# Routed experts in tiles of 512 rows instead of 256, with the down-projection turned round

## The chip, the cores and the metric

The kernel runs on one core of one Trainium2 chip. The metric is the device time of one launch in microseconds (us), lower is better. Times within one core are counted from the first instruction of the profiled execution.

## The reference, cut to what matters

The model has two layers, each with a mixer and a mixture of experts, on x of shape (32, 256, 128) in float32. The change concerns the first layer's experts alone: 8192 tokens of 128 values, 8 experts, each token sent to its two best experts.

```python
x = hidden_states.reshape(-1, H)              # 8192 x 128
logits = x @ gate_w                           # 8 experts
mult, sel = _sparse_mixer_routing(logits)     # two experts a token, a weight for each
w = jnp.sum(mult[:, :, None] * (sel[:, :, None] == jnp.arange(E)[None, None, :]), axis=1)
h = jax.nn.silu(jnp.einsum('th,ehf->etf', x, w1)) * jnp.einsum('th,ehf->etf', x, w3)   # F = 512
out = jnp.einsum('etf,efh,te->th', h, w2, w)
```

## The kernel before

The kernel is a sequence of stages, with a barrier over all engines between them. Four of them bear on the change.

- `ffn_front` computes the router's choices and scatters 16384 rows (two a token, each of 128 values, a destination and a weight) into the table `slot_inputs` in HBM, one region for each expert. GpSimd issues the 128 scatters. The scatter sorts the rows by expert. SyncE writes pad rows, `TOK` of them (256), behind each expert's last row (L871, 8 transfers at addresses that it reads from a table), and `TOK` rows for each tile in excess (L864, 7 transfers). A chain of small VectorE operations on one partition (L1078 to L1095) works out which expert and which row each tile begins at.
- `experts0` runs over a fixed number of tiles of `TOK` rows: `2 * NT // ROWS0` full ones, where NT is 64, and E - 1 = 7 more, because each expert's last tile may be partly empty. With `ROWS0 = 2` that is 64 + 7 = 71 tiles. All of them are computed whether they hold rows or padding.
- `combine0` reads the two results of each token back and adds them to the residual.
- The stages of the second layer follow, and share no code with the change apart from `ROWS0` and `TOK`, which they do not use.

One tile of `experts0` works as follows. SyncE loads its rows (`e_x`, L1132) and its expert's three weight matrices (`e_w`, 768 KB, L1133) up to four tiles ahead. TensorE turns the rows with two transposes (L1151) into PSUM; ScalarE copies them out as `e_xT` (L1190). The hidden width of 512 is worked through in two halves of 256. In each half TensorE multiplies two 128x128 blocks of w1 (L1174) and two of w3 (L1178) with the 256 columns of `e_xT`; ScalarE takes silu of the first (L1197); VectorE multiplies it with the second, giving `e_g` (L1208). In the down-projection (L1161) `e_g` is the stationary operand and a block of w2 the moving one, 128 columns at a time, so that the result has rows on the partitions. VectorE scales it by the row's weight (`e_y`, L1215) and copies the destinations (L1214). GpSimd scatters each 128 rows with an indirect transfer (L1224). The down-projection of a half is emitted one half late, so that TensorE has other work while silu and the product are made. Every engine's order is written out by hand. The waits are on semaphores: `at` and `upto` wait for a count, `upto` on semaphores that start at one.

Of the kernel before, what the change touches and what calls it, by code (L numbers as in the profile page):

```python
# [13 lines left out]
P = 128  # L14
# [626 lines left out]
FC = F // P  # L641
STAGES = 4
CAP = 80
ROWS0 = 2
TOK = ROWS0 * P


# [157 lines left out]
def ffn_front(core, layer, rows, H, XS, background, pad, tables=None, tiles=0):  # L805
# [9 lines left out]
    with on:  # L815
# [26 lines left out]
        with nc.Block() as block:  # L842
# [127 lines left out]
            def _(dve):  # L970
# [99 lines left out]
                if layer == 0:  # L1070
                    step(ts(pad_f[:], base[:], 1.0, None, ALU.add))
                    nc.vector.tensor_copy(pad_row[:], pad_f[0:1, :]).then_inc(S["pad_rows"], 1)
                    expert_of_tile, row_of_tile = tables
                    t1 = lambda name, shape, dt=F32: sb(name, [1, *shape], dt)
                    cnt, cnt_i, ends, step_by = t1("counts", [E]), t1("counts_int", [E], I32), t1("tile_ends", [E]), t1("row_step", [E])
                    tile_no, acc, row, past = t1("tile_no", [tiles]), t1("tile_expert", [tiles]), t1("tile_row", [tiles]), t1("past_end", [E, tiles])

                    step(ts(cnt[:], rev[0:1, :], float(REGION), -float(E * REGION - 1), ALU.mult, ALU.add))  # L1078
                    step(tt(cnt[:], cnt[:], base[0:1, :], ALU.add))
                    step(ts(cnt_i[:], cnt[:], float(TOK - 1), None, ALU.add))  # L1080
                    step(ts(cnt_i[:], cnt_i[:], 8, None, ALU.arith_shift_right))
# [12 lines left out]
                    nc.vector.tensor_copy(expert_of_tile[:], acc[:])  # L1094
                    step(nc.vector.tensor_copy(row_of_tile[:], row[:]))  # L1095


def experts0(core, XS, YS, expert_of_tile, row_of_tile, tiles):

    nc, aps = core.nc, core.aps  # L1100
    U, R3, HALVES = 4, 3, 2
    WIDTH = row_width(0)
    out_rows = YS.shape[0]
    STEPS = tiles * HALVES
    turns = tiles // U
    on = ExitStack()
    with on:
# [1 line left out]
        w = [sb(f"w{n}", [P, 3, FC, P]) for n in range(U)]  # L1109
        x = [sb(f"x{n}", [P, ROWS0, WIDTH]) for n in range(U)]  # L1110
        xT = [sb(f"xT{n}", [P, TOK]) for n in range(2)]
        silu = [sb(f"silu{n}", [P, 2, TOK]) for n in range(2)]
        g = [sb(f"g{n}", [P, 2, TOK]) for n in range(2)]
        y = [sb(f"y{n}", [P, ROWS0, D]) for n in range(R3)]
        idx = [sb(f"idx{n}", [P, ROWS0], U32) for n in range(R3)]
        psX = core.psum("e0_psX", [P, 2, 512], on=on)
        psY = core.psum("e0_psY", [P, 2, 512], on=on)
        ps1, ps3 = (core.psum("e0_ps" + n, [P, 2, 2, TOK], on=on) for n in "13")
        S = start_counts(core, "e0", ["y_ready", "passed"])
        S.update({n: core.sem("e0_" + n) for n in ("xT_ps", "xT_ready", "h1_ps", "h3_ps", "silu_ready", "g_ready", "g_read")})  # L1120
# [4 lines left out]
        with nc.Block() as block:  # L1125
            @block.sync
            def _(sp):
                def emit(q, u):
                    expert = sp.value_load(expert_of_tile[0:1, ds(q, 1)], min_val=0, max_val=E - 1)
                    row = sp.value_load(row_of_tile[0:1, ds(q, 1)], min_val=0, max_val=XS.shape[0] - TOK)  # L1130
                    upto(sp, S["y_ready"], q - U + 1)
                    sp.dma_start(x[u][:], XS[ds(row, TOK), :].rearrange("(p k) w -> p k w", k=ROWS0)).then_inc(x_loaded[u], 16)  # L1132
                    sp.dma_start(w[u][:].rearrange("p k c f -> p (k c f)"), aps["L0_ffn_w_by_expert"][ds(expert, 1)].rearrange("e p f -> p (e f)")).then_inc(w_loaded[u], 16)  # L1133

                for q in range(U):
# [8 lines left out]
            def _(pe):  # L1144
                mm = nc.tensor.matmul

                def turn_in(q):
                    pe.wait_ge(x_loaded[q % U], 16 * (q // U + 1))
                    at(pe, S["xT_ready"], q - 1)
                    for k in range(ROWS0):  # L1150
                        last = nc.tensor.transpose(psX[:, q % 2, k * P:(k + 1) * P], x[q % U][:, k, 0:D], core.ident[:])  # L1151
                    last.then_inc(S["xT_ps"], 1)

                def down(s):
                    q, h = s // HALVES, s % HALVES
                    pe.wait_ge(S["g_ready"], s + 1)
                    if h == 0:
                        upto(pe, S["y_ready"], q - 1)
                    for k in range(ROWS0):
                        for c in range(2):  # L1160
                            last = mm(psY[:, q % 2, k * D:(k + 1) * D], g[s % 2][:, c, k * P:(k + 1) * P], w[q % U][:, 2, 2 * h + c, :],  # L1161
                                      start=(h == 0 and k == 0 and c == 0), stop=(h == 1 and c == 1), skip_group_check=True)
                    last.then_inc(S["g_read"], 1)

                turn_in(0)
                for s in range(STEPS + 1):
                    q, h = s // HALVES, s % HALVES
                    if s < STEPS:
                        if h == 0:
# [3 lines left out]
                        for c in range(2):  # L1173
                            last = mm(ps1[:, s % 2, c, :], w[q % U][:, 0, 2 * h + c, :], xT[q % 2][:], start=True, stop=True)  # L1174
                        last.then_inc(S["h1_ps"], 1)
                        at(pe, S["g_ready"], s - 1)
                        for c in range(2):
                            last = mm(ps3[:, s % 2, c, :], w[q % U][:, 1, 2 * h + c, :], xT[q % 2][:], start=True, stop=True)  # L1178
                        last.then_inc(S["h3_ps"], 1)
                    if h == 0 and q + 1 < tiles:  # L1180
                        turn_in(q + 1)
                    if s >= 1:
                        down(s - 1)

            @block.scalar
            def _(act):
                def turned_in(q):
                    act.wait_ge(S["xT_ps"], q + 1)
                    at(act, S["h3_ps"], HALVES * (q - 1))
                    nc.scalar.activation(xT[q % 2][:], psX[:, q % 2, 0:TOK], ACT.Copy).then_inc(S["xT_ready"], 1)  # L1190

                turned_in(0)
                for s in range(STEPS):
                    q, h = s // HALVES, s % HALVES
                    act.wait_ge(S["h1_ps"], s + 1)
                    at(act, S["g_ready"], s - 1)
                    nc.scalar.activation(silu[s % 2][:], ps1[:, s % 2], ACT.Silu).then_inc(S["silu_ready"], 1)  # L1197
                    if h == 0 and q + 1 < tiles:
                        turned_in(q + 1)

            @block.vector
            def _(dve):
                for s in range(STEPS + 2):
                    if s < STEPS:
                        dve.wait_ge(S["silu_ready"], s + 1)
                        dve.wait_ge(S["h3_ps"], s + 1)
                        at(dve, S["g_read"], s - 1)
                        nc.vector.tensor_tensor(g[s % 2][:], silu[s % 2][:], ps3[:, s % 2], ALU.mult).then_inc(S["g_ready"], 1)  # L1208
                    if s % HALVES == 1 and s >= HALVES:
                        j = s // HALVES - 1  # L1210
                        n = j % R3
                        at(dve, y_stored[n], 16 * ROWS0 * (j // R3))
                        dve.wait_ge(S["g_read"], HALVES * (j + 1))
                        nc.vector.tensor_copy(idx[n][:], x[j % U][:, :, D])  # L1214
                        nc.vector.tensor_tensor(y[n][:], psY[:, j % 2, 0:ROWS0 * D].rearrange("p (k d) -> p k d", d=D),  # L1215
                                                x[j % U][:, :, D + 1].unsqueeze(2).broadcast_to([P, ROWS0, D]), ALU.mult).then_inc(S["y_ready"], 1)

            @block.gpsimd
            def _(pool):
# [1365 lines left out]
```

## Time and profile before

| | us |
|---|---|
| median of 3 runs | 3699.23 |
| lowest and highest | 3692.19 and 3701.08 |
| the profiled execution, its own time | 3701.08 |
| its span, first to last instruction | 3698.9 |

The profiled execution is the highest of the three runs and lies 1.85 us above their median; 2.2 us of its time lie outside the span. Over the whole span TensorE is busy 75%, VectorE 72%, ScalarE 59% and GpSimd 54%. These are averages over stages with different limits. `experts0` takes from about 953 us to about 1356 us of the span, a ninth of it, and what limits it has to be read there. In the profile a float32 matmul shows as two MATMUL instructions and two weight loads (LDWEIGHTS), a transpose as one of each. The record of a matmul is longer than its distance to the next one, since they are pipelined.

### The profile page before, as it was taken

To read this page: it belongs to the slowest core of one execution; us is meant where nothing else is said; L and a number is where in the kernel's file an instruction comes from. 1 tells how busy PE (TensorE), PEld (TensorE's weight loads), DVE (VectorE), ACT (ScalarE), POOL (GpSimd) and SP (SyncE) were. 2 spreads that over 40 slices of the span, in tenths; PEclk is the share of its full clock that TensorE was granted. 3 is DMA by queue.
4 is the path that set the end of the run, shared out by engine and by line. 5 is a ranking of instruction groups with operands and counts; after the bars stand their busy time and mean duration, and the time that the engine had idled before them with its cause. 6 is when DMAs were issued, how large, how long until landed. Compare 5 with 4: busy or idle time off the path is not lost. (4 is left out here: it accounts for less than half of the span.)

```text
span 3698.9 us, 56681 instructions
## 1 busy us (share of the span) xinstructions
PE 2787.0 (75%) x18753; PEld 2111.9 (57%) x18753; DVE 2650.8 (72%) x3627; ACT 2169.2 (59%) x3917; POOL 2005.6 (54%) x1363
## 2 busy tenths in 40 slices
PE   3899999731699950688888888888888887579934
PEld 2455555331599950256666666666666666479833
DVE  3788888444233347179999999999999999867653
ACT  1566666431222210388899898988889988422242
POOL 1111111056333322189999899998999999412234
PEclk9999999755899975799999999999999999889955
DMA  3444444231466665022222222222222222210050
GB/s 93 84 86 91 91 90 88 44 79 47 158 192 192 193 180 117 1 76 81 78 75 78 74 80 75 75 72 75 79 80 77 75 79 82 97 32 23 14 159 15
DMA packets 219478, 321.48 MB, mean 87 GB/s; under 512 B 37210, under 2 KB 132982, under 8 KB 214330
## 3 DMA queue, kind: packets, MB, share of 16 engines
q1 hardware_dynamic: 198914, 299.15, 30.0%
q0 software_dynamic: 12224, 18.29, 1.4%
q8 instruction: 150, 2.46, 0.3%
q10 hardware_dynamic: 8064, 0.55, 0.2%
q14 instruction: 126, 1.03, 0.1%
HBM read 269.80 MB, written 55.68 MB: 88 GB/s over the span
## 5 line engine op out<-in xcount | busy, mean ns | idle before, releaser
L1729 POOL TENSOR_TENSOR resid_x<-s_ux,s_B_rows 128x1024 f32<-128x1024 f32 x256 | 605.3, 2365 | 143.2 <-PE s_y L2089 142.9
L2009 DVE TENSOR_TENSOR_SCAN resid_x<-s_dA,resid_x 128x1024 f32<-128x1024 f32 x256 | 581.7, 2272 | 126.2 <-ACT s_dA L1820 123.3
L2017 DVE TENSOR_TENSOR_SCAN resid_x<-s_back_decay,s_back_in 128x1024 f32<-128x1024 f32 x256 | 584.0, 2281 | 55.2 <-ACT s_back_decay L1830 55.2
L2089 PE MATMUL s_y<-identity,resid_x 128*128 128x128 f32 x4096 | 551.2, 279 | 9.4 <-DVE resid_x L2024 6.3
L2089 PEld LDWEIGHTS s_y<-identity,resid_x 128*128 128x128 f32 x4096 | 491.5, 145 | 60.9 <-issue 28.1
L1737 POOL TENSOR_TENSOR resid_x<-resid_x,s_C_rows 128x1024 f32<-128x1024 f32 x192 | 454.6, 2368 | 3.5 <-DVE resid_x L2009 3.5
L2076 PE MATMUL s_back_in<-identity,resid_x 128*128 128x128 f32 x2048 | 289.7, 287 | 139.6 <-ACT resid_x L1841 71.5
L467 DVE TENSOR_REDUCE a_row_max<-a_maxscores 128x2 f32<-128x512 f32 x512 | 336.2, 683 | 81.4 <-PE a_maxscores L545 80.9
L2024 DVE TENSOR_TENSOR resid_x<-resid_x,s_C 128x1024 f32<-128x1024 f32 x320 | 382.9, 1197 | 10.7 <-PE s_C L2066 10.7
L1820 ACT ACTIVATE s_dA<-s_dt,s_A 128x510 f32<-128x510 f32 x512 | 330.0, 675 | 87.4 <-DVE resid_x L2009 87.0
L1841 ACT ACTIVATE resid_x<-s_uT,s_bT 128x256 f32<-128x256 f32 x864 | 368.8, 497 | 1.3
L391 ACT ACTIVATE a_probs<-a_scores 128x1024 f32<-128x1024 f32 x256 | 262.6, 1026 | 140.8 <-PE a_scores L558 136.2
L1830 ACT ACTIVATE s_back_decay<-s_dt,s_A 128x510 f32<-128x510 f32 x512 | 338.1, 710 | 0.7 <-DVE resid_x L2017 0.7
L2076 PEld LDWEIGHTS s_back_in<-identity,resid_x 128*128 128x128 f32 x2048 | 235.7, 146 | 173.8 <-issue 78.1
L1208 DVE TENSOR_TENSOR e_g<-e_silu,e_ps 128x512 f32<-128x512 f32 x142 | 97.7, 688 | 287.3 <-PE e_ps L1178 286.2
L1224 POOL DMA_INDIRECT choice_outputs<-e_y,e_idx x142 | 137.9, 971 | 270.9 <-DVE e_y L1215 247.0
L2451 PE MATMUL k_psY<-k_coef_T,k_basis 128*128 128x128 f32 x2048 | 237.6, 277 | 19.4 <-DVE k_basis L2399 19.4
L2111 PE MATMUL s_prep<-s_xT,s_w_taps 128*128 128x512 f32 x512 | 233.9, 599 | 20.4 <-ACT s_bT L1930 14.9
L2451 PEld LDWEIGHTS k_psY<-k_coef_T,k_basis 128*128 128x128 f32 x2048 | 233.6, 194 | 22.4 <-DVE k_basis L2399 13.4
L545 PE MATMUL a_maxscores<-a_K,a_Q 72*128 72x256 bf16 x1024 | 207.5, 287 | 41.1 <-DVE a_row_max L467 29.9
L1197 ACT ACTIVATE e_silu<-e_ps 128x512 f32<-128x512 f32 x142 | 84.8, 597 | 241.3 <-PE e_ps L1174 236.5
L378 POOL TENSOR_TENSOR a_qk_cos<-a_qk,a_cos 128x512 f32<-128x512 f32 x32 | 40.8, 1275 | 312.4 <-ACT a_qk L413 312.4
(327 smaller groups left out, 5443.6 us busy)
## 6 DMA issues: line engine op xcount, KB each, us to landing
s_B_rows<-forward_rows SPq DMA_DIRECT2D x256, 256.0 KB, 3.3
e_w<-L_ffn_w_by_expert SPq DMA_DIRECT2D x71, 768.0 KB, 4.5
s_C_rows<-forward_rows SPq DMA_DIRECT2D x192, 256.0 KB, 3.4
a_Q<-split_qk SPq DMA_DIRECT2D x96, 192.0 KB
split_qk<-a_parts SPq DMA_DIRECT2D x32, 384.0 KB, 2.8
e_x<-slot_inputs SPq DMA_DIRECT2D x71, 130.0 KB
a_K<-split_qk SPq DMA_DIRECT2D x64, 128.0 KB
f_mod_rows<-mod_rows SPq DMA_DIRECT2D x16, 512.0 KB, 10.1
```

Source lines behind the costliest of these rows:

```text
L467: nc.vector.tensor_reduce(mx[b % 2][:, h, :], MX[:, h % 2], AX.X, ALU.max).then_inc(S["max_done"], 1)
L1729: tt(R[s, 0], ux[par][:], brow[s % BRING][:].unsqueeze(1).broadcast_to([P, C2, W]), ALU.mult).then_inc(S["in_ready"], 1)
L1737: tt(r, r, crow[k % CRING][:].unsqueeze(1).broadcast_to([P, C2, W]), ALU.mult).then_inc(S["part_pool"], 1)
L1820: last = func(dA[:, c2, :, 1:T], dt[par][:, 0, c2, :].rearrange("p (g t) -> p g t", t=T)[:, :, 1:T], ACT.Exp, scale=Wt["A"][:, 0, c2, s:s ...
L1830: last = func(dec[s % 2][:, c2, :, 0:T - 1], dt[par][:, 1, c2, :].rearrange("p (g t) -> p g t", t=T)[:, :, 0:T - 1], ACT.Exp, scale=Wt["A" ...
L1841: last = func(bt[s % 2][:, k, :], uT[par][:, k, :], ACT.Identity, scale=bT[par][:, k, s:s + 1])
L2009: nc.vector.tensor_tensor_scan(r, a, r, 0.0, ALU.mult, ALU.add).then_inc(S["scanned"], 1)
L2017: nc.vector.tensor_tensor_scan(r[:, ::-1], a[:, ::-1], b[:, ::-1], 0.0, ALU.mult, ALU.add).then_inc(S["scanned"], 1)
L2024: tt(r, r, CP[:].unsqueeze(1).broadcast_to([P, C2, W]), ALU.mult).then_inc(S["part_dve"], 1)
L2076: last = nc.tensor.transpose(bP[:, c2, k // TC, (k % TC) * P:(k % TC + 1) * P], bt[s % 2][:, k, c2 * P:(c2 + 1) * P], core.ident[:])
L2089: last = mm(YP[:, t, c2 * P:(c2 + 1) * P], R[s, d][:, c2, t * P:(t + 1) * P], core.ident[:], is_transpose=True, start=((s, d) == (0, 1) an ...
L2451: last = nc.tensor.matmul(psY[:, n, k * D:(k + 1) * D], basis[n][:, m, k * P:(k + 1) * P], WT[:, m, :], start=(m == 0), stop=(m == NBASIS ...
```

## The change

`ROWS0` goes from 2 to 4, so that a tile has 512 rows; the count of full tiles becomes 32 and that of all tiles 39. The hidden width is worked through in four chunks of 128 instead of two halves of 256, each chunk with one matmul of 512 columns for w1 and one for w3. The down-projection has its operands exchanged: w2's block is stationary and `g` moving, one matmul of 512 columns for each chunk, emitted two chunks late. Its result has the 128 output values on the partitions (`psY`). ScalarE copies it out (`yT`), and TensorE turns it back with four transposes (`turn_out`) into a new PSUM tile `psZ`, from which VectorE makes `y`. `psX` has one buffer instead of two, and so has `psZ`; `silu` has three and `g` four. GpSimd issues four scatters a tile instead of two. SyncE waits for `yT_ready` before it loads a tile's weights, because w2 is now read up to the matmul that `yT` waits for.

```diff
-ROWS0 = 2
+ROWS0 = 4
...
-                    step(ts(cnt_i[:], cnt_i[:], 8, None, ALU.arith_shift_right))
+                    step(ts(cnt_i[:], cnt_i[:], 9, None, ALU.arith_shift_right))
...
-    STEPS = tiles * HALVES
+    CHUNKS = tiles * FC
...
-        silu = [sb(f"silu{n}", [P, 2, TOK]) for n in range(2)]
-        g = [sb(f"g{n}", [P, 2, TOK]) for n in range(2)]
+        silu = [sb(f"silu{n}", [P, TOK]) for n in range(R3)]
+        g = [sb(f"g{n}", [P, TOK]) for n in range(4)]
+        yT = [sb(f"yT{n}", [P, TOK]) for n in range(2)]
...
-        psX = core.psum("e0_psX", [P, 2, 512], on=on)
-        psY = core.psum("e0_psY", [P, 2, 512], on=on)
-        ps1, ps3 = (core.psum("e0_ps" + n, [P, 2, 2, TOK], on=on) for n in "13")
+        psX, psZ = (core.psum("e0_ps" + n, [P, ROWS0, P], on=on) for n in "XZ")
+        ps1, ps3, psY = (core.psum("e0_ps" + n, [P, 2, TOK], on=on) for n in "13Y")
...
                     sp.dma_start(x[u][:], XS[ds(row, TOK), :].rearrange("(p k) w -> p k w", k=ROWS0)).then_inc(x_loaded[u], 16)
+                    upto(sp, S["yT_ready"], q - U + 1)
                     sp.dma_start(w[u][:].rearrange("p k c f -> p (k c f)"), aps["L0_ffn_w_by_expert"][ds(expert, 1)].rearrange("e p f -> p (e f)")).then_inc(w_loaded[u], 16)
...
+                def turn_out(q):
+                    upto(pe, S["yT_ready"], q + 1)
+                    upto(pe, S["y_ready"], q)
+                    for k in range(ROWS0):
+                        last = nc.tensor.transpose(psZ[:, k, :], yT[q % 2][:, k * P:(k + 1) * P], core.ident[:])
+                    last.then_inc(S["z_ps"], 1)
+
                 def down(s):
-                    q, h = s // HALVES, s % HALVES
+                    q, c = s // FC, s % FC
                     pe.wait_ge(S["g_ready"], s + 1)
-                    if h == 0:
-                        upto(pe, S["y_ready"], q - 1)
-                    for k in range(ROWS0):
-                        for c in range(2):
-                            last = mm(psY[:, q % 2, k * D:(k + 1) * D], g[s % 2][:, c, k * P:(k + 1) * P], w[q % U][:, 2, 2 * h + c, :],
-                                      start=(h == 0 and k == 0 and c == 0), stop=(h == 1 and c == 1), skip_group_check=True)
-                    last.then_inc(S["g_read"], 1)
+                    if c == 0:
+                        upto(pe, S["yT_ready"], q - 1)
+                    mm(psY[:, q % 2, :], w[q % U][:, 2, c, :], g[s % 4][:], start=(c == 0), stop=(c == FC - 1)).then_inc(S["y_chunk"], 1)
 
                 turn_in(0)
+                for s in range(CHUNKS + FC):
+                    q, c = s // FC, s % FC
+                    if s < CHUNKS:
+                        if c == 0:
                             pe.wait_ge(w_loaded[q % U], 16 * (q // U + 1))
                             pe.wait_ge(S["xT_ready"], q + 1)
                         at(pe, S["silu_ready"], s - 1)
+                        mm(ps1[:, s % 2, :], w[q % U][:, 0, c, :], xT[q % 2][:], start=True, stop=True).then_inc(S["h1_ps"], 1)
                         at(pe, S["g_ready"], s - 1)
+                        mm(ps3[:, s % 2, :], w[q % U][:, 1, c, :], xT[q % 2][:], start=True, stop=True).then_inc(S["h3_ps"], 1)
+                    if 0 <= s - 2 < CHUNKS:
+                        down(s - 2)
+                    if c == 2 and q + 1 < tiles:
                         turn_in(q + 1)
+                    if c == 3 and 0 <= q - 1:
+                        turn_out(q - 1)
...
+                for s in range(CHUNKS + 2):          # ScalarE
+                    q, c = s // FC, s % FC
+                    if s < CHUNKS:
+                        act.wait_ge(S["h1_ps"], s + 1)
+                        at(act, S["g_ready"], s - R3 + 1)
+                        nc.scalar.activation(silu[s % R3][:], ps1[:, s % 2, :], ACT.Silu).then_inc(S["silu_ready"], 1)
+                    if c == 1 and q >= 1:
+                        act.wait_ge(S["y_chunk"], FC * q)
+                        at(act, S["z_ps"], q - 2)
+                        nc.scalar.activation(yT[(q - 1) % 2][:], psY[:, (q - 1) % 2, :], ACT.Copy).then_inc(S["yT_ready"], 1)
+                    if c == 2 and q + 1 < tiles:
                         turned_in(q + 1)
...
+                for s in range(CHUNKS + FC + 1):     # VectorE
+                    q, c = s // FC, s % FC
+                    if s < CHUNKS:
                         dve.wait_ge(S["silu_ready"], s + 1)
                         dve.wait_ge(S["h3_ps"], s + 1)
+                        at(dve, S["y_chunk"], s - 3)
+                        nc.vector.tensor_tensor(g[s % 4][:], silu[s % R3][:], ps3[:, s % 2, :], ALU.mult).then_inc(S["g_ready"], 1)
+                    if c == 0 and q >= 2:
+                        j, n = q - 2, (q - 2) % R3
                         at(dve, y_stored[n], 16 * ROWS0 * (j // R3))
+                        dve.wait_ge(S["z_ps"], j + 1)
                         nc.vector.tensor_copy(idx[n][:], x[j % U][:, :, D])
+                        nc.vector.tensor_tensor(y[n][:], psZ[:], x[j % U][:, :, D + 1].unsqueeze(2).broadcast_to([P, ROWS0, D]), ALU.mult).then_inc(S["y_ready"], 1)
```

## Rows read from the trace of the kernel before

**Rows 1.** Stretches: length, busy us of each engine (instructions), PE clock, DMA share, GB/s.

```profile
950.00:960.00 10.00, 3.15 (x8) 2.30 (x9) 0.00 (x0) 2.02 (x3) 0.00 (x0) 0.50 0.59 185
1000.00:1100.00 100.00, 100.00 (x625) 91.56 (x623) 32.47 (x73) 28.99 (x55) 34.96 (x36) 1.00 0.61 195
```

**Rows 2.** Waits in the stretch 953:1352: total us, times, longest.

```profile
PE e_ps L1174 <- DMA e_w<-L_ffn_w_by_expert: 1.8, 1, 1.8
```

**Rows 3.** Groups by line, 953:1352: count, busy us, mean ns, idle before.

```profile
L1161 PE MATMUL e_psY<-e_w,e_g 128*128 128x128 f32 x1136 | 149.9, 275 | 0.0
L1161 PEld LDWEIGHTS e_psY<-e_w,e_g 128*128 128x128 f32 x1136 | 143.7, 192 | 3.9
L1224 POOL DMA_INDIRECT choice_outputs<-e_y,e_idx x142 | 137.9, 971 | 270.9 <-DVE e_y L1215 247.0 <-issue 23.9
L1208 DVE TENSOR_TENSOR e_g<-e_silu,e_ps 128x512 f32<-128x512 f32 x142 | 97.7, 688 | 287.3 <-PE e_ps L1178 286.2 <-ACT e_silu L1197 1.1
L1197 ACT ACTIVATE e_silu<-e_ps 128x512 f32<-128x512 f32 x142 | 84.8, 597 | 241.3 <-PE e_ps L1174 236.5 <-issue 2.8 <-DVE e_g L1208 2.0
L1214 DVE CAST e_idx<-e_x 128x2 uint32<-128x2 f32 x71 | 11.5, 162 | 0.9 <-PE e_psY L1161 0.9
```

**Rows 4.** Timeline of TensorE over one tile: start, length of merged group, count.

```profile
1100.22 1.03 PE L1174 MATMUL e_ps<-e_xT,e_w 128*128 128x256 f32 x4
1101.09 1.03 PE L1178 MATMUL e_ps<-e_xT,e_w 128*128 128x256 f32 x4
1101.95 0.38 PE L1151 MATMUL e_psX<-identity,e_x 128*128 128x128 f32 x2
1102.17 1.06 PE L1161 MATMUL e_psY<-e_w,e_g 128*128 128x128 f32 x8
1103.06 1.03 PE L1174 MATMUL e_ps<-e_xT,e_w 128*128 128x256 f32 x4
```

**Rows 5.** Timeline of SyncE: transfers of rows, one a tile.

```profile
1199.15 0.33 SPq L1132 DMA_DIRECT2D e_x<-slot_inputs  x1
...
1210.06 0.34 SPq L1132 DMA_DIRECT2D e_x<-slot_inputs  x1
```

**Rows 6.** Timeline of TensorE in the second layer's mixer: matmuls of 512 columns.

```profile
1648.51 3.60 PE L2111 MATMUL s_prep<-s_xT,s_w_taps 128*128 128x512 f32 x8
1651.95 0.38 PE L2066 MATMUL s_C<-s_bc_parts,s_w_sel 96*128 96x512 bf16 x1
```

**Rows 7.** Group by line: a ScalarE copy of 512 columns out of PSUM, in attention.

```profile
L431 ACT ACTIVATE a_out_sums<-a_out 128x512 f32<-128x512 f32 x32 | 18.9, 592 | 2.5 <-PE a_out L572 2.4
```

**Rows 8.** Timeline at the stage's end.

```profile
1344.85 2.16 PE L1161 MATMUL e_psY<-e_w,e_g 128*128 128x128 f32 x16
1345.78 0.42 DVE L1215 TENSOR_TENSOR e_y<-e_psY,e_x 128x256 f32<-128x256 f32 x1
1346.97 0.97 POOL L1224 DMA_INDIRECT choice_outputs<-e_y,e_idx  x1 [2.99 <-DVE e_y L1215]
...
1350.80 0.97 POOL L1224 DMA_INDIRECT choice_outputs<-e_y,e_idx  x1 [0.30 <-issue]
1356.00 0.34 SPq L1246 DMA_DIRECT2D c_gate<-mod_rows  x1
```

**Rows 9.** Timeline around the stage's start, pad rows first.

```profile
915.62 33.26 SPq L871 DMA_DIRECT2D slot_inputs<-f_pad_rows  x8
...
952.84 0.37 SPq L1132 DMA_DIRECT2D e_x<-slot_inputs  x1
...
957.54 2.07 PE L1174 MATMUL e_ps<-e_xT,e_w 128*128 128x256 f32 x4 [1.81 <-DMA e_w<-L_ffn_w_by_expert]
...
960.86 0.38 PE L1151 MATMUL e_psX<-identity,e_x 128*128 128x128 f32 x2
```

**Rows 10.** DMA issues: count, KB each, median us to landing.

```profile
s_B_rows<-forward_rows SPq DMA_DIRECT2D x256, 256.0 KB, 3.3
e_w<-L_ffn_w_by_expert SPq DMA_DIRECT2D x71, 768.0 KB, 4.5
```

More of the change, by code:

```diff
@@ L1100, in experts0 @@
     nc, aps = core.nc, core.aps
-    U, R3, HALVES = 4, 3, 2
+    U, R3 = 4, 3
     WIDTH = row_width(0)
     out_rows = YS.shape[0]
-    STEPS = tiles * HALVES
+    CHUNKS = tiles * FC
     turns = tiles // U
@@ L1111, in experts0 @@
         xT = [sb(f"xT{n}", [P, TOK]) for n in range(2)]
-        silu = [sb(f"silu{n}", [P, 2, TOK]) for n in range(2)]
-        g = [sb(f"g{n}", [P, 2, TOK]) for n in range(2)]
+        silu = [sb(f"silu{n}", [P, TOK]) for n in range(R3)]
+        g = [sb(f"g{n}", [P, TOK]) for n in range(4)]
+        yT = [sb(f"yT{n}", [P, TOK]) for n in range(2)]
         y = [sb(f"y{n}", [P, ROWS0, D]) for n in range(R3)]
         idx = [sb(f"idx{n}", [P, ROWS0], U32) for n in range(R3)]
-        psX = core.psum("e0_psX", [P, 2, 512], on=on)
-        psY = core.psum("e0_psY", [P, 2, 512], on=on)
-        ps1, ps3 = (core.psum("e0_ps" + n, [P, 2, 2, TOK], on=on) for n in "13")
-        S = start_counts(core, "e0", ["y_ready", "passed"])
-        S.update({n: core.sem("e0_" + n) for n in ("xT_ps", "xT_ready", "h1_ps", "h3_ps", "silu_ready", "g_ready", "g_read")})
+        psX, psZ = (core.psum("e0_ps" + n, [P, ROWS0, P], on=on) for n in "XZ")
+        ps1, ps3, psY = (core.psum("e0_ps" + n, [P, 2, TOK], on=on) for n in "13Y")
+        S = start_counts(core, "e0", ["yT_ready", "y_ready", "passed"])
+        S.update({n: core.sem("e0_" + n) for n in ("xT_ps", "xT_ready", "h1_ps", "h3_ps", "silu_ready", "g_ready", "y_chunk", "z_ps")})
         w_loaded = [core.sem(f"e0_w_loaded{u}") for u in range(U)]
@@ L1148, in turn_in @@
                     pe.wait_ge(x_loaded[q % U], 16 * (q // U + 1))
-                    at(pe, S["xT_ready"], q - 1)
+                    at(pe, S["xT_ready"], q)
                     for k in range(ROWS0):
-                        last = nc.tensor.transpose(psX[:, q % 2, k * P:(k + 1) * P], x[q % U][:, k, 0:D], core.ident[:])
+                        last = nc.tensor.transpose(psX[:, k, :], x[q % U][:, k, 0:D], core.ident[:])
                     last.then_inc(S["xT_ps"], 1)
+                def turn_out(q):
[4 more added lines that the diff above has]
+                    last.then_inc(S["z_ps"], 1)
                 def down(s):
-                    q, h = s // HALVES, s % HALVES
+                    q, c = s // FC, s % FC
                     pe.wait_ge(S["g_ready"], s + 1)
-                    if h == 0:
-                        upto(pe, S["y_ready"], q - 1)
-                    for k in range(ROWS0):
-                        for c in range(2):
-                            last = mm(psY[:, q % 2, k * D:(k + 1) * D], g[s % 2][:, c, k * P:(k + 1) * P], w[q % U][:, 2, 2 * h + c, :],
-                                      start=(h == 0 and k == 0 and c == 0), stop=(h == 1 and c == 1), skip_group_check=True)
-                    last.then_inc(S["g_read"], 1)
+                    if c == 0:
+                        upto(pe, S["yT_ready"], q - 1)
+                    mm(psY[:, q % 2, :], w[q % U][:, 2, c, :], g[s % 4][:], start=(c == 0), stop=(c == FC - 1)).then_inc(S["y_chunk"], 1)
                 turn_in(0)
[L1166 to L1169, printed above, removed]
+                for s in range(CHUNKS + FC):
+                    q, c = s // FC, s % FC
+                    if s < CHUNKS:
+                        if c == 0:
                             pe.wait_ge(w_loaded[q % U], 16 * (q // U + 1))
@@ L1172, in _ @@
                         at(pe, S["silu_ready"], s - 1)
-                        for c in range(2):
-                            last = mm(ps1[:, s % 2, c, :], w[q % U][:, 0, 2 * h + c, :], xT[q % 2][:], start=True, stop=True)
-                        last.then_inc(S["h1_ps"], 1)
+                        mm(ps1[:, s % 2, :], w[q % U][:, 0, c, :], xT[q % 2][:], start=True, stop=True).then_inc(S["h1_ps"], 1)
                         at(pe, S["g_ready"], s - 1)
[L1177 to L1180, printed above, removed]
+                        mm(ps3[:, s % 2, :], w[q % U][:, 1, c, :], xT[q % 2][:], start=True, stop=True).then_inc(S["h3_ps"], 1)
+                    if 0 <= s - 2 < CHUNKS:
+                        down(s - 2)
+                    if c == 2 and q + 1 < tiles:
                         turn_in(q + 1)
-                    if s >= 1:
-                        down(s - 1)
+                    if c == 3 and 0 <= q - 1:
+                        turn_out(q - 1)
             @block.scalar
@@ L1188, in turned_in @@
                     act.wait_ge(S["xT_ps"], q + 1)
-                    at(act, S["h3_ps"], HALVES * (q - 1))
-                    nc.scalar.activation(xT[q % 2][:], psX[:, q % 2, 0:TOK], ACT.Copy).then_inc(S["xT_ready"], 1)
+                    at(act, S["h3_ps"], FC * (q - 1))
+                    nc.scalar.activation(xT[q % 2][:], psX[:].rearrange("p k t -> p (k t)"), ACT.Copy).then_inc(S["xT_ready"], 1)
                 turned_in(0)
[L1193 to L1198, printed above, removed]
+                for s in range(CHUNKS + 2):
[9 more added lines that the diff above has]
+                    if c == 2 and q + 1 < tiles:
                         turned_in(q + 1)
@@ L1202, in _ @@
             def _(dve):
-                for s in range(STEPS + 2):
-                    if s < STEPS:
+                for s in range(CHUNKS + FC + 1):
+                    q, c = s // FC, s % FC
+                    if s < CHUNKS:
                         dve.wait_ge(S["silu_ready"], s + 1)
                         dve.wait_ge(S["h3_ps"], s + 1)
[L1207 to L1211, printed above, removed]
+                        at(dve, S["y_chunk"], s - 3)
+                        nc.vector.tensor_tensor(g[s % 4][:], silu[s % R3][:], ps3[:, s % 2, :], ALU.mult).then_inc(S["g_ready"], 1)
+                    if c == 0 and q >= 2:
+                        j, n = q - 2, (q - 2) % R3
                         at(dve, y_stored[n], 16 * ROWS0 * (j // R3))
-                        dve.wait_ge(S["g_read"], HALVES * (j + 1))
+                        dve.wait_ge(S["z_ps"], j + 1)
                         nc.vector.tensor_copy(idx[n][:], x[j % U][:, :, D])
-                        nc.vector.tensor_tensor(y[n][:], psY[:, j % 2, 0:ROWS0 * D].rearrange("p (k d) -> p k d", d=D),
-                                                x[j % U][:, :, D + 1].unsqueeze(2).broadcast_to([P, ROWS0, D]), ALU.mult).then_inc(S["y_ready"], 1)
+                        nc.vector.tensor_tensor(y[n][:], psZ[:], x[j % U][:, :, D + 1].unsqueeze(2).broadcast_to([P, ROWS0, D]), ALU.mult).then_inc(S["y_ready"], 1)
             @block.gpsimd
```

## The prediction

> **What bounds the kernel now.** I read the busy time by stretches first. All the changed work lies in the expert stage, and inside it TensorE is busy for the whole of every 100 us, at the full clock of 2.4 GHz, while VectorE and ScalarE are busy a third of it [rows 1]. A busy TensorE need not be a full one, since records of pipelined matmuls overlap, so I looked at what it waited for: in the whole stage only the transfers at its very start, once for weights, 1.8 us [rows 2]. The groups by line show no idle time ahead of its matmuls there, but long idle times on the other engines, all ended by TensorE's work [rows 3]. So the stage is a queue of matmuls with no gap, and its length is what TensorE's queue holds. The reader should take from this that weights' traffic, silu, products and scatters cost nothing now, and that making them fewer gains nothing.
>
> The next question is what a matmul costs: its columns, or itself. The timeline of one tile gives distances between starts. Four MATMULs of 256 columns take 1101.09 - 1100.22 = 0.87 us, 217 ns each; eight of 128 columns take 1103.06 - 1102.17 = 0.89 us, 111 ns each; a transpose takes 110 ns [rows 4]. Eight of 512 columns, in the mixer, take 1651.95 - 1648.51 = 3.44 us, 430 ns each [rows 6]. Per column that is 0.87, 0.85 and 0.84 ns. The price is by columns, with some 4 ns for each instruction: matmuls twice as wide save almost nothing.
>
> As a check, a tile now has 8 matmuls of 256 columns and 8 of 128, each two MATMULs, and two transposes: 16 x 0.217 + 16 x 0.111 + 2 x 0.110 = 5.47 us. The row transfers of tiles two apart are (1210.06 - 1199.15) = 10.91 us apart, 5.455 us a tile [rows 5]. 71 tiles are 387.3 us.
>
> **The change part by part.**
>
> *TensorE's queue.* A tile of 512 rows has 8 up and 4 down matmuls of 512 columns, so 24 MATMULs x 430 ns = 10.32 us; four transposes in and four out, 8 x 110 ns = 0.88 us. Together 11.20 us. Two old tiles, the same number of rows, take 10.91 us. So the matmuls' columns are the same (per 512 rows 6144 before and after), the wide form saves about 0.15 us, and the turn back costs 4 x 110 = 0.44 us: a tile's worth of rows becomes 0.29 us dearer.
>
> *Tiles.* 39 tiles of 512 rows compute 19968 rows, 71 of 256 computed 18176, for 16384 real ones. This is the larger part: the seven tiles in excess are twice as large. 39 x 11.20 = 436.8 us against 387.3 us. From the first up matmul to the last down matmul, leave out the first tile's transposes on both sides (0.22 before; 0.44 after) and the last turn back (0.44, counted with the drain): 435.9 - 387.1 = **+48.8 us**. The slow clock at the start is the same on both sides: it stood at 0.50, 1.2 GHz, after TensorE had been idle, and the first eight MATMULs took 960.86 - 957.54 = 3.3 us instead of 1.7 [rows 1, 9]. I leave it out.
>
> *Does TensorE stay full?* Times from the start of a new tile, for chunks of 3 x 0.86 = 2.58 us. Silu of a chunk starts when its first matmul is out (about 1.05: its second MATMUL starts at 0.43, and (3.60 - 7 x 0.430) = 0.59 is the record of one [rows 6]) and takes 0.60; the product starts at about 1.95 and takes 0.69, done at 2.64 [rows 3]. The down matmul that needs it starts two chunks later, at 5.16 + 1.72 = 6.9, the buffers are wanted by the matmuls from 5.16 on: over 2.5 us to spare. The new ScalarE copies take 0.59 us each [rows 7]. `yT` follows the last down matmul of the previous tile, which leaves the queue at 5.16; it is done at about 5.9 and wanted at 10.76. ScalarE waits there in front of the next silu, but that one can't start before 6.2. `xT` follows the transposes at 8.18, is done at about 9.0 and wanted at 11.20; the silu behind it can't start before 9.25. `psZ` is read by VectorE after the product of the first chunk, from 2.64 to about 3.5 (0.16 for the indices, 0.69 for a product of this size); it is next written at 10.76, and the next product can't start before 4.5. ScalarE works 4 x 0.60 + 2 x 0.59 = 3.6 us of 11.2, VectorE 3.6. GpSimd issues four scatters, 4 x 1.28 = 5.1 us (the distance of the scatters at the end, (1350.80 - 1346.97) / 3 [rows 8]). The loads are issued when a tile four back is done, which leaves over 15 us for the rows and 18 for the weights, where these land in 4.5 us [rows 10]; the added wait on SyncE is for `yT_ready`, always passed before the `y_ready` ahead of it. Traffic of weights falls from 71 to 39 x 768 KB, which gives nothing, as it is hidden. So I cost all waits at nothing. The cover of the nearest one, `xT`, is about 2 us.
>
> *The drain.* Before, the last down matmul leaves the queue at 1344.85 + 16 x 0.111 = 1346.6. The last-but-one tile's `y` is done at 1346.20, GpSimd starts 0.77 us later and issues 2 + 2 scatters until 1351.8, 5.1 us after TensorE; the next stage's first transfer follows at 1356.0 [rows 8]. After: TensorE turns the last-but-one tile back before its last two down matmuls, at 1.7 us before the end E of its queue. `y` is done at about E - 0.8, GpSimd starts at about E, and its four scatters last until E + 5.1. The last tile goes down matmul, copy (0.8), transposes (1.5), `y` (2.3): before E + 5.1, so its four scatters follow directly, until E + 10.2. **+5.1 us.**
>
> *The front.* The pad rows and the extra tiles' rows are 15 transfers of twice the size (260 KB). The last eight are issued from 915.6 over 33 us, and the stage opens at 952.8, so the last one is on the path [rows 9]. For its landing the nearest rows are 256 KB in 3.3 us and 768 KB in 4.5 [rows 10], 0.24 us for 100 KB: +0.3 us. The first tile's rows are also doubled and lie ahead of its weights: +0.5 us with the transfers that share the engines. Bounds: nothing, and 3 us if every queue behind them shifts. **+0.8 us.** The tables' operations get shorter (39 for 71 columns), in cover of the scatters.
>
> **The sum:** 48.8 + 5.1 + 0.8 = +54.7 us. Against the profiled execution's 3701.08 that is 3755.8; against the median of 3699.23, 3753.9. I say 3755.
>
> **Rivals.**
>
> *Wide matmuls come cheaper (ends faster).* A weight load of the down-projection has a record of 192 ns, longer than the 111 ns between its matmuls, and weight loads fill 91.6 of 100 us [rows 1, 3]. If they were what TensorE is full of, the fall from 68 to 32 of them per 512 rows would decide. With drain and front at +5.9 us the change gains below a distance of 371 ns for 512 columns: (387.3 - 5.9) / 39 = 9.78 us a tile, (9.78 - 0.88) / 24. If only the loads counted, at 111 ns each, a tile would take 32 x 0.111 = 3.6 us, VectorE and GpSimd's scatters would then bound it at 5.1 us, 39 x 5.1 = 199 us in place of 387: with the 5.9 us about 3519. Against it speak the 430 ns of the mixer, the same weight shape and type at the same clock. Chance 0.03.
>
> The Trainium skill speaks for that rival: in "TensorE: Matmul & The Clock Gate", section "Back-to-back issue gap", it puts the sustained distance of matmuls at about 81 ns for 128 columns and 131 for 512, 1.6 times for four times the columns. By that ratio a MATMUL of 512 would take an estimated 180 ns here, and 39 tiles of 24 x 0.18 + 0.88 = 5.2 us some 203 us. The trace disagrees: 430 to 111 ns is 3.9 times [rows 4, 6].
>
> *The hand-overs don't fit (slower still).* `psX` and `psZ` have one buffer, and ScalarE's queue holds two waits on TensorE in front of silus. If one of them stalls TensorE at each tile by a copy and its hand-overs, about 1 us, that is 39 us: 3794. Against it: the 2 us or more that I count at each. Chance 0.07.
>
> *Pad transfers set their own pace (slower).* The eight of them are spread over 33 us with nothing in the rows that explains it. If bytes do it, twice as large ones take up to 33 us more: 3788. Against it: 33 us for eight is 4 us each, and transfers of twice this size land in 3.3 us [rows 10], so bytes alone don't take that long. Chance 0.04.
>
> *The change is covered (no change).* TensorE would have to have some 50 us of room in the stage; it has 2 us. Chance 0.01.
>
> **How the numbers follow.** My forecast has 0.85. Its own range comes from the tile's price, 11.1 to 11.3 us (4 us either way), the front (up to 3 us), the drain (2 us) and the spread of the runs before, 9 us: 3747 to 3765. The rivals above it take 0.11 and the ones below 0.04; extending it somewhat towards stalls of a few tenths of a us a tile gives 3746 to 3768. A measurement of this kernel tells about 0.3%, 11 us, from no change. Faster 0.03, same 0.01, slower 0.96.
>
> **What would show it.** Right: in the expert stage TensorE still without waits, row transfers 11.2 us apart, 39 of them; MATMULs of 512 columns 430 ns apart; the stage's last scatter about 10 us behind the last down matmul; everything from the next stage on shifted by some 55 us and as long as before. Wrong: waits of TensorE for `yT`, `xT` or `y`, a granted clock under 1.00 in the stage's middle, distances under 400 ns, or a first row transfer later than about 954 us.

## The result, and the profile after

The changed kernel takes 3761.27 us in the median (3751.95 to 3763.06, 4 runs) against 3698.22 us (3692.19 to 3701.08, 4 runs): a ratio of 1.0161, 95% interval 1.0143 to 1.0177. It is slower, within the range predicted. The profiled execution took 3750.54 us, with a span of 3748.5 us. Further executions of the changed kernel lay between 3747.87 and 3763.73 us, so a single profile can't stand for the median to better than some 8 us, and what follows compares the stage, not the spans.

First the stretches inside the expert stage, of the changed kernel (length, busy us of TensorE, its weight loads, VectorE, ScalarE and GpSimd, granted clock, DMA share, GB/s). They answer to [rows 1].

```profile
1000.00:1100.00 100.00, 100.00 (x288) 47.82 (x287) 30.81 (x54) 31.71 (x54) 34.98 (x36) 1.00 0.34 116
1200.00:1300.00 100.00, 100.00 (x288) 47.88 (x287) 30.21 (x53) 32.24 (x54) 35.04 (x36) 1.00 0.34 116
```

TensorE is as full as before. Its instructions fell from 625 to 288 in 100 us, its weight loads' busy time from 91.6 to 47.8 us, the weights' traffic from 195 to 116 GB/s, and none of this shortened the stage. The waits of TensorE from before the stage to its end (total us, times, longest) are the two at its start and one in the drain, that is, behind the last down matmul; the first is for the most part the time before the stage opens.

```profile
PE e_psX L1152 <- DMA e_x<-slot_inputs: 45.9, 1, 45.9
PE e_ps L1177 <- DMA e_w<-L_ffn_w_by_expert: 0.9, 1, 0.9
PE e_psZ L1159 <- ACT e_yT L1204: 0.7, 1, 0.7
```

The timeline of TensorE over one tile (start, length of the merged group, count), to be read beside [rows 4]:

```profile
1197.04 1.02 PE L1177 MATMUL e_ps<-e_xT,e_w 128*128 128x512 f32 x2
1197.90 1.02 PE L1179 MATMUL e_ps<-e_xT,e_w 128*128 128x512 f32 x2
1198.76 1.02 PE L1167 MATMUL e_psY<-e_g,e_w 128*128 128x512 f32 x2
1199.62 1.02 PE L1177 MATMUL e_ps<-e_xT,e_w 128*128 128x512 f32 x2
...
1204.77 0.60 PE L1152 MATMUL e_psX<-identity,e_x 128*128 128x128 f32 x4
1205.21 1.02 PE L1177 MATMUL e_ps<-e_xT,e_w 128*128 128x512 f32 x2
...
1207.79 0.60 PE L1159 MATMUL e_psZ<-identity,e_yT 128*128 128x128 f32 x4
1208.22 1.02 PE L1177 MATMUL e_ps<-e_xT,e_w 128*128 128x512 f32 x2
```

A pair of MATMULs of 512 columns takes 0.86 us, four transposes 0.44 us, and the tile 1208.22 - 1197.04 = 11.18 us. Row transfers, the answer to [rows 5], are 11.18 us apart.

```profile
1222.91 0.33 SPq L1132 DMA_DIRECT2D e_x<-slot_inputs  x1
...
1234.09 0.33 SPq L1132 DMA_DIRECT2D e_x<-slot_inputs  x1
```

The stage's start and end in the timeline, beside [rows 8, 9]:

```profile
920.38 32.73 SPq L871 DMA_DIRECT2D slot_inputs<-f_pad_rows  x8
957.50 0.37 SPq L1132 DMA_DIRECT2D e_x<-slot_inputs  x1
...
962.41 2.07 PE L1177 MATMUL e_ps<-e_xT,e_w 128*128 128x512 f32 x2 [0.91 <-DMA e_w<-L_ffn_w_by_expert]
...
1397.82 1.88 PE L1167 MATMUL e_psY<-e_g,e_w 128*128 128x512 f32 x4
1398.16 0.68 DVE L1222 TENSOR_TENSOR e_y<-e_psZ,e_x 128x512 f32<-128x512 f32 x1
1399.62 0.97 POOL L1230 DMA_INDIRECT choice_outputs<-e_y,e_idx  x1 [3.63 <-DVE e_y L1222]
...
1401.22 0.68 DVE L1222 TENSOR_TENSOR e_y<-e_psZ,e_x 128x512 f32<-128x512 f32 x1
...
1408.56 0.97 POOL L1230 DMA_INDIRECT choice_outputs<-e_y,e_idx  x1 [0.30 <-issue]
1415.13 0.34 SPq L1252 DMA_DIRECT2D c_gate<-mod_rows  x1
```

The stage, from its first row transfer to the next stage's first transfer, takes 1415.13 - 957.50 = 457.6 us, before 1356.00 - 952.84 = 403.2: +54.5 us. Here are its parts, with the stretch ahead of it in the first line, each a difference of two starts or ends in the rows above and in [rows 8, 9].

| us | before | after | change | forecast |
|---|---|---|---|---|
| first pad transfer to stage's opening | 37.2 | 37.1 | -0.1 | +0.3 |
| opening to first up matmul | 4.7 | 4.9 | +0.2 | +0.5 |
| first up matmul to end of the queue | 389.1 | 437.1 | +48.0 | +48.8 |
| end of the queue to end of the last scatter | 5.1 | 10.0 | +4.9 | +5.1 |
| last scatter to next stage's first transfer | 4.2 | 5.6 | +1.4 | 0 |

The end of the queue is the last group's start with 0.430 us for each of its four MATMULs (0.111 for sixteen before). Outside, the changed execution came 4.8 us later to the pad transfers and went 9.5 us faster through everything behind the stage; the code there is the same in the two kernels, but for the size of seven pad transfers. That is why the spans differ by 49.6 us only. The 4.8 us does not go with the size of the tile: the first of the eight pad transfers starts at 909.5 us in one kernel of 512-row tiles below (copies twice) and at 919.1 in one of 256 (turned, small tiles). In the first 500 us the mean granted clock was 0.90 here and 0.99 in the profile before; how much of the 4.8 us that is was not tried. The medians differ by 63 us; the interval of the ratio, 53 to 65 us, contains 54.5.

### The profile page after: what moved, and what is told of

Same layout as the page of the kernel before. It is cut to its first block and busy times, and to the rows that moved or that the text cites. A ratio compares the mean times of both kernels' runs of the same rounds, so it can differ in the third digit from the quotient of the medians.

```text
span 3748.5 us, 53813 instructions
## 1 busy us (share of the span) xinstructions
PE 2838.7 (76%) x17587; PEld 1970.4 (53%) x17587; DVE 2656.1 (71%) x3577; ACT 2197.5 (59%) x3938; POOL 2021.0 (54%) x1377
## 5 line engine op out<-in xcount | busy, mean ns | idle before, releaser
L2095 PEld LDWEIGHTS s_y<-identity,resid_x 128*128 128x128 f32 x4096 | 495.0, 145 | 59.5 <-issue 37.1
L1216 DVE TENSOR_TENSOR e_g<-e_silu,e_ps 128x512 f32<-128x512 f32 x156 | 107.3, 688 | 328.3 <-PE e_ps L1179 281.5
L1230 POOL DMA_INDIRECT choice_outputs<-e_y,e_idx x156 | 151.8, 973 | 310.5 <-DVE e_y L1222 273.0
L1200 ACT ACTIVATE e_silu<-e_ps 128x512 f32<-128x512 f32 x156 | 93.2, 597 | 192.8 <-PE e_ps L1177 183.6
```

The costliest lines, as they stand in the source:

```text
L2095: last = mm(YP[:, t, c2 * P:(c2 + 1) * P], R[s, d][:, c2, t * P:(t + 1) * P], core.ident[:], is_transpose=True, start=((s, d) == (0, 1) an ...
```

## The experiments

Every run is compared with runs of the kernel before on its own chip, and chips differ (the kernel before had medians from 3651 to 3707 us), so only ratios are compared across runs. The stage's length is read from each profile as above; the one profile of the kernel before stands for it in all comparisons of lengths. "Queue" is here from the start of the first up matmul to the start of the last down MATMUL.

| kernel | tiles x rows | stage | queue | ratio to before, 95% interval |
|---|---|---|---|---|
| before | 71 x 256 | 403.2 | 389.2 | 1 |
| changed | 39 x 512 | 457.6 | 436.7 | 1.0161 (1.0143 to 1.0177) |
| old down-projection | 39 x 512 | 444.1 | 426.4 | 1.0117 (1.0096 to 1.0138) |
| turned, small tiles | 71 x 256 | 415.6 | 400.4 | 1.0035 (1.0020 to 1.0049) |
| 37 tiles | 37 x 512 | 435.0 | 414.7 | 1.0072 (1.0052 to 1.0092) |
| copies twice | 39 x 512 | 458.6 | 437.3 | 1.0144 (1.0127 to 1.0161) |
| tiles of 128 | 135 x 128 | 442.1 | 430.6 | 1.0098 (1.0072 to 1.0125) |
| before, fewer loads | 71 x 256 | 404.5 | 389.9 | 1.0002 (0.9988 to 1.0016) |
| tiles of 128, fewer loads | 135 x 128 | 402.2 | 390.7 | 1.0002 (0.9989 to 1.0014) |
| the same, five buffers | 135 x 128 | 391.0 | 379.6 | 0.9973 (0.9960 to 0.9987) |

**The old down-projection in tiles of 512 rows.** One part of the change undone; `yT`, the transposes back and `psZ` go with it, and VectorE makes `y` from `psY`.

```diff
-                    mm(psY[:, q % 2, :], w[q % U][:, 2, c, :], g[s % 4][:], start=(c == 0), stop=(c == FC - 1)).then_inc(S["y_chunk"], 1)
+                    for k in range(ROWS0):
+                        last = mm(psY[:, q % 2, k * D:(k + 1) * D], g[s % 4][:, k * P:(k + 1) * P], w[q % U][:, 2, c, :],
+                                  start=(c == 0 and k == 0), stop=(c == FC - 1), skip_group_check=True)
+                    last.then_inc(S["y_chunk"], 1)
```

> Tiles of 512 rows as in the changed kernel, but the down-projection in its old form (g stationary, 128 columns moving), so no copy of yT, no transposes back. By columns: 16 MATMULs x 0.430 + 32 x 0.111 + 4 x 0.110 = 10.87 us a tile instead of 11.18, and the last tile's scatters start about 3 us sooner. Against the changed kernel -15 us, of which -12 in TensorE's queue; against the kernel before +39 us (ratio about 1.011). If the hand-overs of yT and psZ cost TensorE time beyond its columns, the gain is larger than 15 us; if the turned form's wide matmuls save more than I counted, this kernel is slower than the changed one.

Its stage is 13.5 us shorter than the changed kernel's (15 expected), its queue 10.3 us (12 expected). In its timeline a chunk's down-projection is eight narrow MATMULs again, and a tile takes 1209.21 - 1198.33 = 10.88 us.

```profile
1198.33 1.02 PE L1171 MATMUL e_ps<-e_xT,e_w 128*128 128x512 f32 x2
1199.19 1.02 PE L1173 MATMUL e_ps<-e_xT,e_w 128*128 128x512 f32 x2
1200.05 1.05 PE L1159 MATMUL e_psY<-e_w,e_g 128*128 128x128 f32 x8
1200.94 1.02 PE L1171 MATMUL e_ps<-e_xT,e_w 128*128 128x512 f32 x2
...
1209.21 1.02 PE L1171 MATMUL e_ps<-e_xT,e_w 128*128 128x512 f32 x2
```

Eight narrow MATMULs take 0.89 us where the two wide ones take 0.86. The wide form wins 4 x 0.03 = 0.12 us a tile and pays 0.44 us for turning back, 0.32 us lost. The two tiles differ by 11.18 - 10.88 = 0.30 us, so no cost of the hand-overs comes on top.

**The turned form in tiles of 256 rows.** The other part alone: `ROWS0 = 2`, a shift by 8, and each PSUM buffer given its own 512 columns.

```diff
-ROWS0 = 4
+ROWS0 = 2
...
-        ps1, ps3, psY = (core.psum("e0_ps" + n, [P, 2, TOK], on=on) for n in "13Y")
+        ps1, ps3, psY = (core.psum("e0_ps" + n, [P, 2, 512], on=on)[:, :, 0:TOK] for n in "13Y")
```

> The turned down-projection with tiles of 256 rows (71 tiles). By columns: 24 MATMULs x 0.217 + 4 x 0.110 = 5.65 us a tile against 5.455: 71 x 0.195 = +14 us against the kernel before, with no cost for tiles in excess, a ratio of about 1.004. If the hand-overs are what costs, they cost more here, since chunks are half as long (1.3 us) and there are 71 of them: a stall of 0.5 us a tile would give +50 us.

The ratio is 1.0035 against the 1.004 expected. The stage is 12.4 us longer than the kernel before's. A tile takes 1202.28 - 1196.65 = 5.63 us, and TensorE has no wait in it although chunks are half as long.

```profile
1196.65 0.60 PE L1177 MATMUL e_ps<-e_xT,e_w 128*128 128x256 f32 x2
...
1202.28 0.60 PE L1177 MATMUL e_ps<-e_xT,e_w 128*128 128x256 f32 x2
```

**Two tiles fewer.** The routing of these inputs fills 37 tiles of 512 rows; this kernel leaves out the last two of the list, which hold padding. With other inputs it would leave out rows.

```diff
-    tiles = used + E - 1
+    tiles = used + E - 3
```

> The changed kernel with 37 tiles in place of 39; the routing of these inputs fills 37, and the two left out hold padding alone. If each tile in excess costs its full TensorE time, 2 x 11.18 = -22 us against the changed kernel (ratio to the kernel before about 1.010). If excess tiles were cheap and the turned form dear, -5 us or less.

The stage is 22.6 us shorter than the changed kernel's, the queue 22.0. An empty tile costs what a full one does.

**Copies made twice.** ScalarE's two new hand-overs are made longer.

```diff
+                    nc.scalar.activation(twice[q % 2][:, 0, :], psX[:].rearrange("p k t -> p (k t)"), ACT.Copy)
                     nc.scalar.activation(xT[q % 2][:], psX[:].rearrange("p k t -> p (k t)"), ACT.Copy).then_inc(S["xT_ready"], 1)
...
+                        nc.scalar.activation(twice[(q - 1) % 2][:, 1, :], psY[:, (q - 1) % 2, :], ACT.Copy)
                         nc.scalar.activation(yT[(q - 1) % 2][:], psY[:, (q - 1) % 2, :], ACT.Copy).then_inc(S["yT_ready"], 1)
```

> The changed kernel with ScalarE making each of its copies xT and yT twice, the first time into an unused tile: 1.2 us more ScalarE work a tile, and each hand-over 0.6 us later. By my count of 2 us of cover, no change in the stage (under 1 us). By the rival of hand-overs that don't fit, 0.6 to 1.2 us for each of 39 tiles: +23 to +47 us, and TensorE shows waits for yT or xT.

The queue is 437.3 us long against 436.7, the stage 458.6 against 457.6: +1.0, where under 1 us was expected. It lies at the start: from the opening to the first up matmul 0.4 us, and 0.6 in the first three tiles, which take 33.4, 33.7 and 34.0 us in the changed kernel, the one of 37 tiles and this one. Later tiles are 11.18 us apart as before. In its stretches ScalarE works 38.87 us of 100 instead of 31.71, TensorE is full, with as many instructions. The second copy starts 0.5 us behind the first, so each hand-over grew by 0.5 us rather than 0.6.

```profile
1000.00:1100.00 100.00, 100.00 (x288) 47.88 (x287) 30.81 (x54) 38.87 (x72) 34.97 (x36) 1.00 0.34 116
...
1197.11 0.60 ACT L1193 ACTIVATE e_twice<-e_psX 128x512 f32<-128x512 f32 x1 [1.44 <-PE e_psX L1153]
1197.60 0.59 ACT L1194 ACTIVATE e_xT<-e_psX 128x512 f32<-128x512 f32 x1
```

The rival of hand-overs that don't fit is ruled out: each could be 0.5 us later still and TensorE would not notice.

**Tiles of 128 rows.** If excess rows are the price, smaller tiles should pay. The kernel before with `ROWS0 = 1` and a shift by 7.

```diff
-ROWS0 = 2
+ROWS0 = 1
...
-        ps1, ps3 = (core.psum("e0_ps" + n, [P, 2, 2, TOK], on=on) for n in "13")
+        ps1, ps3 = (core.psum("e0_ps" + n, [P, 2, 2, 256], on=on)[:, :, :, 0:TOK] for n in "13")
```

> The kernel before with tiles of 128 rows: 128 + 7 = 135 tiles, 17280 rows computed instead of 18176, the two forms otherwise unchanged. By TensorE's columns alone 24 MATMULs x 0.111 + 0.110 = 2.77 us a tile, 135 x 2.77 = 374 us: -13 us against the kernel before. But each tile still loads 768 KB of weights: 135 x 0.9 MB = 124 MB, where the kernel before moves 195 GB/s at a DMA share of 0.61, so some 320 GB/s at most: 388 us; and SyncE needs about 2.2 us a tile to read its table and issue. If the weights' traffic takes over, the stage is 390 to 450 us and TensorE waits for w_loaded: 0 to +60 us.

The stage came out at 442.1 us, +38.9. TensorE now waits in the middle of the stage, 24.4 us for weights and 6.4 for rows (the 43.8 us below is the time before the stage opens), and the transfers run at 284 to 296 GB/s over 100 us with a DMA share near 0.9.

```profile
PE e_psX L1151 <- DMA e_x<-slot_inputs: 50.2, 18, 43.8
PE e_ps L1174 <- DMA e_w<-L_ffn_w_by_expert: 24.4, 38, 2.8
...
1000.00:1100.00 100.00, 90.81 (x775) 87.60 (x775) 34.26 (x124) 32.33 (x93) 30.13 (x31) 1.00 0.89 286
```

I had expected up to 320 GB/s from the kernel before's share; it stopped below 300. That need not be all that the transfers can do: while the changed kernel fills its first buffers they run at 374 GB/s.

```profile
960.00:970.00 10.00, 8.70 (x17) 4.08 (x18) 1.50 (x3) 3.67 (x5) 0.00 (x0) 0.68 0.98 374
```

Every load waits for the `y` of the tile four before, so a late load can mean too little rate or too little head start. No run loads for every tile with more buffers; the loads hold this kernel back, and which of the two it is stays open. That it is the loads, and not SyncE's time, the next runs show.

**Loading weights only where the expert changes.** The rows are sorted by expert, so a buffer often holds the right weights already. VectorE marks in the table the tiles whose expert is that of the tile four before, and SyncE branches.

```diff
+                    step(tt(same[:, 4:tiles], acc[:, 4:tiles], acc[:, 0:tiles - 4], ALU.is_equal))
+                    step(nc.vector.memset(same[:, 0:4], 0.0))
+                    step(stt(out=same[:], in0=same[:], scalar=float(E), in1=acc[:], op0=ALU.mult, op1=ALU.add))
...
+                        with sp.If(expert < E):
+                            load()
+                        with sp.Else():
+                            sp.sem_inc(w_loaded[u], 16)
```

In the kernel before, with its tiles of 256 rows:

> The kernel before, tiles of 256 rows, with the same skipping of weight loads whose expert is already in the buffer: some 30 of 71 loads or more fall away. If the weights' traffic is hidden at this tile size, no change: the stage 403 us, ratio 1.000 within 0.2%. If it costs TensorE anything (slower matmuls through shared memory ports, late loads), the stage gets shorter by what it costs.

The ratio is 1.0002, the queue 389.9 us. 32 loads are left of 71, four for each expert. The DMA share falls from 0.61 to 0.36 and TensorE's row is the same as in [rows 1] within 3 instructions.

```profile
1000.00:1100.00 100.00, 100.00 (x622) 91.51 (x621) 32.03 (x72) 28.99 (x55) 35.61 (x37) 1.00 0.36 112
```

So the weights' traffic is hidden at 256 rows. In tiles of 128 rows:

> Tiles of 128 rows as in the run before, but SyncE reloads a weight buffer only where its expert changes: the table marks tiles whose expert is that of the tile four before, and a branch skips their 768 KB. With the traffic gone TensorE's columns should bind again: 135 x 2.77 = 374 us for the queue, the stage near 388 us instead of 403 in the kernel before: -15 us, ratio about 0.996. If SyncE's own time is what held the 128-row tiles back (two reads, a branch, one or two issues, near 3 us a tile), the stage stays over 405 us and TensorE waits for the rows' transfers.

This expectation was wrong: 1.0002, not 0.996, and not for SyncE's time. The queue shrank from 430.6 to 390.7 us, but steady tiles would make 377: GpSimd's scatters, one a tile, start at 1204.24, 1207.04 and 1209.82, 2.79 us apart. Most of the rest are waits where an expert changes and four loads come in a row; the next run takes 11.1 us of it away.

```profile
1217.39 0.71 PE L1185 MATMUL e_ps<-e_xT,e_w 128*128 128x128 f32 x4 [0.30 <-DMA e_w<-L_ffn_w_by_expert]
1220.92 0.71 PE L1185 MATMUL e_ps<-e_xT,e_w 128*128 128x128 f32 x4 [0.48 <-DMA e_w<-L_ffn_w_by_expert]
```

**Five buffers.** The same with `U = 5`, and the tile five before in the table.

```diff
-    U, R3, HALVES = 4, 3, 2
+    U, R3, HALVES = 5, 3, 2
```

> Tiles of 128 rows with loads only where the expert changes, now with five weight and row buffers instead of four. In the run with four, steady tiles were 2.79 us apart (135 x 2.79 = 377 us), but the queue took 390.7 us, the rest being waits for weights where four loads follow one another at each change of expert. One buffer more issues each load one tile (2.8 us) earlier, against waits of at most 1.9 us there: the queue near 378 us, the stage 389 to 391 us against 403 in the kernel before, a ratio of about 0.9965. If the rate of the loads sets it regardless of the head start (five loads in a row now), the stage stays at 402 us.

The queue is 379.6 us long, the stage 391.0, 12.2 less than the kernel before's, and the ratio 0.9973 with an interval of 0.9960 to 0.9987. It is faster than both kernels, though by less than the 0.3% that I called the resolution of a few runs; this comparison had 12 and 17. TensorE is full, with hardly a gap between weight loads. Here a buffer more, that is an earlier issue, was enough, so the rate of the loads did not set the pace in this kernel.

```profile
1000.00:1100.00 100.00, 100.00 (x899) 100.00 (x898) 39.81 (x144) 37.66 (x108) 34.49 (x37) 1.00 0.41 127
```

## Why the prediction was right

**The bound.** That TensorE's queue is the stage holds in every kernel with tiles of 256 or 512 rows: no waits inside, and lengths that follow columns. Two experiments moved what was said to be free and found it free (loads skipped, copies doubled).

**The price by columns.** 512 columns cost 430 ns here as in the mixer [rows 6]; the tile was forecast at 11.20 us and is 11.18, which is the 0.8 us by which the queue came out shorter than forecast. The rival of cheap wide matmuls fell. The ratio that "TensorE: Matmul & The Clock Gate" of the Trainium skill gives under "Back-to-back issue gap", 1.6 for four times the columns, does not hold for these float32 matmuls: the kernels here show 0.86 us for two wide against 0.89 for eight narrow, so 430 ns against 111 for one, 3.9 times. The bf16 MATMUL of 512 columns in [rows 6] starts at 1651.95 and the one behind it at 1652.17, so it takes 0.22 us, half of a float32 one.

```profile
1652.17 0.60 PE L2089 MATMUL s_y<-identity,resid_x 128*128 128x128 f32 x4
```

**The split.** I put the larger part on tiles in excess. The measured queue grows by 48.0 us. Turning back costs 0.30 us a tile, 39 x 0.30 = 12 us, and the run without it has a queue 10.3 us shorter. The rest, 37 to 38 us, is rows: 19968 against 18176, at 10.88 / 512 us a row 38 us. The two parts were tried apart and add up: the turned form alone +11.2 us of queue at 71 tiles, large tiles alone (old form) 426.4 - 389.2 = +37.2 us, together 48.4 against 47.5 measured in the same way, from the first start to the last start.

**The hand-overs.** Counted at about 2 us of cover; the timeline has `xT` done at 1206.01 and the next tile at 1208.22, 2.2 us later.

```profile
1205.41 0.60 ACT L1192 ACTIVATE e_xT<-e_psX 128x512 f32<-128x512 f32 x1 [1.56 <-issue]
```

**The drain.** +5.1 forecast, +4.9 measured, by the mechanism named: eight scatters in a row behind the queue.

**The front.** Nothing instead of +0.3, and +0.2 instead of +0.5 behind the opening. Doubling the pad transfers' bytes left their 33 us as they were (32.73), and halving them in tiles of 128 rows too (32.52), so the rival of a pace set by bytes is out. Nor is it a property of the code: in the kernel before with fewer loads, profiled on another chip, the same eight transfers of the same size are issued in 8.28 us, in the midst of the scatters, and the stage opens at 930.38, 5.4 us behind the end of the last scatter of `ffn_front` (925.02). So the pad transfers were on the path in the profiles of the result and not in that one. What sets their pace stays open.

```profile
851.44 8.28 SPq L871 DMA_DIRECT2D slot_inputs<-f_pad_rows  x8
```

**A sign that misled.** A first row transfer later than about 954 us was to count against the forecast. It came at 957.50, though the stretch from the pad transfers to the opening was no longer than before: that execution was 4.8 us late before it began. An absolute time in one execution was a poor sign; the difference of two events in it would have been a good one.

**What was missed.** The last scatter to the next stage took 1.4 us more. From the last scatter's start it is 6.6 us in kernels of 39 tiles of 512 rows, 5.9 with 37 tiles, 5.2 with 256 rows and 4.6 to 4.7 with 128. It grows with the tile, but not simply with the scatters that follow one another at the end: with 37 tiles there are eight of them as with 39. No run tested it and the cause stays open. So the near agreement of the stage's sum, +54.5 measured and 48.8 + 5.1 + 0.5 = +54.4 forecast, is partly luck: the terms were 1.3 us too large together, and 1.4 us was missing. And my range took 9 us for the spread of runs from three of them; twelve executions of the changed kernel spread over 16 us. The median of 3761 lies 6 us above my 3755, which is within that spread.

## What to carry to other kernels

Where TensorE has no gaps, ask only what is added to its queue, in columns: fewer instructions, fewer weight loads and less traffic gave nothing here, wider matmuls next to nothing (0.12 us of an 11 us tile), and a transpose back had to be paid in full. In an expert layer with a fixed number of tiles, E - 1 of them are there for rounding and cost as much as full ones, so the tile size is a price, and its lower limit is set by what each tile loads. If a small tile is held back by reloading the same weights, skip the reload and add a buffer for the bursts, and measure the burst, not the average.

## What the runs showed of the hardware

- A float32 MATMUL follows the last by 111, 217 and 430 ns for 128, 256 and 512 columns at the full clock, for 128 columns in both operand orders. With 128 columns throughout, the records of the weight loads, 192 ns each, overlap and fill 100 of 100 us, and the MATMULs still follow one another by 111 ns (899 in 100 us).
- Loads of 768 KB for every tile of 128 rows, with rows and scatters beside them, ran at 284 to 296 GB/s over 100 us at a DMA share of 0.87 to 0.91. The first loads of the changed kernel ran at 374 GB/s at a share of 0.98.
- Two ScalarE copies of 512 columns in a row start 0.5 us apart, though each has a record of 0.6.
- A branch on SyncE around a load, with two table reads a tile, kept up with a tile each 2.79 us.
